# Moving a sub-block's preparation from VectorE to ScalarE and GpSimd in a row-by-row triangular solve

## What is computed

```python
probs = jax.nn.softmax(logits + causal_mask, axis=-1)
L = jnp.eye(s, dtype=probs.dtype) - jnp.tril(probs, -1)
rhs = jnp.diagonal(probs, axis1=-2, axis2=-1)[..., None] * v
A = jax.scipy.linalg.solve_triangular(L, rhs, lower=True)
```

## Time and profile before

| what | value |
|---|---|
| median of 3 runs | 1405.09 us (1400.81 to 1409.5) |
| profiled execution | 1403.81 us, span 1401.9 us |
| the four solve blocks, from the span's start | 596 to 713, 809 to 924, 1041 to 1156, 1242 to 1358 us: 463 us |
| VectorE busy in these 463 us | 388.1 us |
| TensorE busy in these 463 us | 338.8 us |
| GpSimd busy in these 463 us | 111.1 us |

### The profile page before, as it was taken

The page is one execution under the profiler, slowest core; times in us unless marked ns, Lnnn a source line. Parts: engine busy times, 40 slices in busy tenths (PEclk is TensorE's granted clock), DMA queues, the critical chain, the costliest instruction groups (busy, mean ns, idle before and its releaser), DMA issues. The chain is left out here.

```text
span 1401.9 us, 29590 instructions
## 1 busy us (share of the span) xinstructions
PE 981.4 (70%) x10762; PEld 766.5 (55%) x10762; DVE 900.0 (64%) x3559; ACT 466.1 (33%) x1066; POOL 341.8 (24%) x390
## 2 busy tenths in 40 slices
PE   5376599970665056877769968769986777986754
PEld 5165499960621034666545657646665655775643
DVE  5656262216789065888768888758878970058857
ACT  1233244424224003311235411235532126941215
POOL 1277154540047170021210021210001230012221
PEclk9788799995579587966889966789977788987877
DMA  9397598836018864410034220044411005411008
GB/s 220 46 209 210 155 249 238 228 95 180 26 50 237 244 151 123 113 28 20 21 97 129 77 61 20 22 110 125 114 46 36 24 21 163 136 45 38 28 22 235
DMA packets 241824, 153.95 MB, mean 110 GB/s; under 512 B 80432, under 2 KB 226096, under 8 KB 241424
## 3 DMA queue, kind: packets, MB, share of 16 engines
q1 hardware_dynamic: 232528, 133.04, 37.0%
q0 software_dynamic: 9152, 19.02, 4.2%
HBM read 96.76 MB, written 55.24 MB: 108 GB/s over the span
## 5 line engine op out<-in xcount | busy, mean ns | idle before, releaser
L1157 DVE TENSOR_REDUCE mx<-banks 128x1 f32<-128x384 f32 (+3 forms) x352 | 203.3, 634 | 72.6 <-PE banks L1088 72.0
L1323 DVE TENSOR_TENSOR prod<-A,Kst_Pn 128x8 f32<-128x8 f32 (+30 forms) x992 | 179.4, 221 | 0.6
L1329 DVE TENSOR_REDUCE A<-prod 128x4 f32<-128x8 f32 (+30 forms) x992 | 174.8, 217 | 0.0
L800 POOL DMA_INDIRECT o_dram<-step_o,step_to x80 | 81.4, 1017 | 309.4 <-ACT step_o L789 297.2
L1137 ACT ACTIVATE Eoff<-banks 128x256 f32<-128x256 f32 (+2 forms) x192 | 114.9, 598 | 102.6 <-PE banks L1073 93.6
L1071 PE MATMUL banks<-Qexp,Kst_Pn 128*128 128x256 bf16 x640 | 115.5, 282 | 44.1 <-DMA Qmax<-q_stack 34.0
L1139 ACT ACTIVATE Ed<-banks 128x256 f32<-128x256 f32 x256 | 98.0, 383 | 111.4 <-PE banks L1073 111.4
L1084 PE MATMUL banks<-masks,identb 128*128 128x128 bf16 (+2 forms) x352 | 90.3, 256 | 59.8 <-DMA Qmax<-q_stack 50.9
L1088 PE MATMUL banks<-Kst_Pn,Qmax 128*128 128x128 bf16 (+3 forms) x512 | 123.3, 313 | 0.0
L756 PE MATMUL banks<-step_xT,step_w 128*128 128x256 f32 x320 | 105.8, 488 | 22.5 <-issue 22.0
L1263 POOL TENSOR_TENSOR A<-A,Kst_Pn 128x256 f32<-128x256 f32 x16 | 19.4, 1213 | 408.0 <-DVE Kst_Pn L1293 408.0
(11 more groups left out here) (197 smaller groups left out, 1816.0 us busy)
## 6 DMA issues: line engine op xcount, KB each, us to landing
Kst_Pn<-k_stack SPq DMA_DIRECT2D x32, 512.0 KB, 4.6
rows_dram<-blank SPq DMA_DIRECT2D x12, 858.0 KB, 12.1
e_w<-in_L_w1T_dram SPq DMA_DIRECT2D x39, 256.0 KB
e_w<-in_L_w2T_dram SPq DMA_DIRECT2D x39, 256.0 KB
Qmax<-q_stack SPq DMA_DIRECT2D x64, 96.0 KB
Qexp<-q_stack SPq DMA_DIRECT2D x64, 96.0 KB
Kst_Pn<-k_stack SPq DMA_DIRECT2D x16, 384.0 KB, 4.5
step_xt<-rows_dram SPq DMA_DIRECT2D x40, 132.0 KB, 2.2
```

Source lines behind the costliest of these rows:

```text
L800: self.nc.gpsimd.indirect_dma_start(self.o_dram, bass.IndirectOffsetOnAxis(self.to[n][:, j:j + 1], 0), self.o[n][:, j, :], None).then_inc( ...
L1157: nc.vector.tensor_reduce(out, logits, AX_X, ALU.max, negate=True).then_inc(max_done, 1)
L1323: nc.vector.tensor_tensor(prod[:, ds, 0:r + 1], A[:, ds, k0:k0 + r + 1], Pn[:, c * SUB + r:c * SUB + r + 1, 0:r + 1].broadcast_to([P, HD / ...
L1329: nc.vector.tensor_reduce(A[:, ds, k0 + r], prod[:, ds, 0:r + 1], AX_X, ALU.add).then_inc(row_done, 1)
```

## The change

Sub-block 0 of each block is still prepared by VectorE (`first_terms`). For sub-blocks 1 to 3 the preparation is handed over: ScalarE copies the turned probabilities unscaled into `Pn` (`keep_probs`, ahead of its expert steps of the sub-block before), and GpSimd's `prepare(c + 1)`, ahead of its sends of sub-block c, makes `term`, scales all of `Pn` in one instruction of 128x1024 elements, does the own term and adds `term` to `A`. VectorE keeps the transposes and the reciprocals, but does each `turn_before` one sub-block earlier: that of sub-block 1 ahead of the rows of sub-block 0, that of c + 1 behind `keep_rows(c - 1)`. Its sums of earlier sub-blocks now go through `later` in place. New semaphores are `probs_kept` (ScalarE to TensorE and GpSimd) and `z_done` (VectorE to GpSimd). `before` and `term` have one buffer each, so VectorE waits for `own_done` before it overwrites `before`.

```diff
 def turn_next(c):
     for g in range(per_sub * c, per_sub * (c + 1)):
-        if g >= 2:
-            pe.wait_ge(probs_in, g - 1)
+        if g < 2 * per_sub:
+            pe.wait_ge(probs_in, g - per_sub + 1)
+        else:
+            pe.wait_ge(probs_kept, g - 2 * per_sub + 1)
...
 def _(act):
+    def keep_probs(c):
+        for g in range(per_sub * c, per_sub * (c + 1)):
+            act.wait_ge(probs_turned, g)
+            nc.scalar.copy(Pn[:, g * TURN:(g + 1) * TURN, :],
+                           bank[g % 2][:, 0:TURN * SUB].rearrange("p (q k) -> p q k", k=SUB)).then_inc(probs_kept, 1)
+
     for c in range(NSUB):
+        if c + 1 < NSUB:
+            keep_probs(c + 1)
         for k in tiles[c]:
...
 def _(pool):
+    own = Chain(pool, own_done)
...
+    def own_term(c):
+        ts = slice(t0 + c * SUB, t0 + (c + 1) * SUB)
+        own(nc.gpsimd.tensor_tensor(A[:, :, ts], A[:, :, ts],
+                                    diagonal(c).rearrange("p (a i) -> p a i", a=1).broadcast_to([P, HD, SUB]), ALU.mult))
+        own(nc.gpsimd.memset(diagonal(c), 1.0))
+
+    def prepare(c):
+        qs, ts = slice(c * SUB, (c + 1) * SUB), slice(t0 + c * SUB, t0 + (c + 1) * SUB)
+        z = rZ[:, qs].rearrange("p (q a) -> p q a", a=1)
+        pool.wait_ge(z_done, c)
+        own(nc.gpsimd.tensor_tensor(term[:, :, :], before[:, :, 0:HD].rearrange("p q d -> p d q"),
+                                    rZ[:, qs].rearrange("p (a q) -> p a q", a=1).broadcast_to([P, HD, SUB]), ALU.mult))
+        pool.wait_ge(probs_kept, per_sub * c)
+        own(nc.gpsimd.tensor_tensor(Pn[:, qs, :], Pn[:, qs, :], z.broadcast_to([P, SUB, SUB]), ALU.mult))
+        own_term(c)
+        own(nc.gpsimd.tensor_tensor(A[:, :, ts], A[:, :, ts], term[:, :, :], ALU.add))
+
+    pool.wait_ge(probs_in, per_sub)
+    own_term(0)
     for c in range(NSUB):
...
+        if c + 1 < NSUB:
+            prepare(c + 1)
         for k in tiles[c]:
             steps.send(pool, k)
...
 def add_later(c):
     dve.wait_ge(later_mm, c)
     base(nc.vector.transpose(later[:, :, :], wide[:, 0:SUB * HD].rearrange("p (t d) -> p d t", d=HD)))
-    add_term(c, later[:, :, :])
+    dve.wait_ge(z_done, c)
+    add_term(c, later[:, :, :], later[:, :, :], 2 + 5 * c)
+
+turn_before(0)
+first_terms()
+turn_before(1)
 for c in range(NSUB):
-    turn_before(c)
     if c:
         keep_rows(c - 1)
-    add_before(c)
-    if c:
+        if c + 1 < NSUB:
+            dve.wait_ge(own_done, 2 + 5 * c)
+            turn_before(c + 1)
         add_later(c)
-    dve.wait_ge(own_done, 2 * c + 2)
```

More of the change, by code:

```diff
@@ L1191, in solve_block @@
         sb, sem = tensors(nc, ctx)
-        own_done, base_done = sem("own_done"), sem("base_done")
+        own_done, base_done, probs_kept, z_done = sem("own_done"), sem("base_done"), sem("probs_kept"), sem("z_done")
         probs_turned, probs_in = sem("probs_turned"), sem("probs_in")
@@ L1257, in _, with diagonal @@
         def _(pool):
-            for c in range(NSUB):
[L1259 to L1266, removed]
+            own = Chain(pool, own_done)
+            def diagonal(c):
+                first = c * SUB * SUB
+                return Pn.rearrange("p q k -> p (q k)")[:, first:first + (SUB - 1) * (SUB + 1) + 1:SUB + 1]
+            def own_term(c):
[15 more added lines that the diff above has]
+            own_term(0)
+            for c in range(NSUB):
+                if c + 1 < NSUB:
+                    prepare(c + 1)
                 for k in tiles[c]:
@@ L1274, in _, with add_term, first_terms @@
             base = Chain(dve, base_done)
-            def add_term(c, sums):
+            def add_term(c, sums, out, ready):
                 qs = slice(c * SUB, (c + 1) * SUB)
                 ts = slice(t0 + c * SUB, t0 + (c + 1) * SUB)
[L1279 to L1282, removed]
+                base(nc.vector.tensor_tensor(out, sums, rZ[:, qs].rearrange("p (a q) -> p a q", a=1).broadcast_to([P, HD, SUB]), ALU.mult))
+                dve.wait_ge(own_done, ready)
+                base(nc.vector.tensor_tensor(A[:, :, ts], A[:, :, ts], out, ALU.add))
             def turn_before(c):
                 base(nc.vector.transpose(before[:, :, :], RT[:, c, :, :].rearrange("p t q -> p q t")))
-                base(nc.vector.reciprocal(rZ[:, c * SUB:(c + 1) * SUB], before[:, :, HD]))
-            def add_before(c):
-                for g in range(per_sub * c, per_sub * (c + 1)):
+                if c:
+                    nc.vector.reciprocal(rZ[:, c * SUB:(c + 1) * SUB], before[:, :, HD]).then_inc(z_done, 1)
+                else:
+                    base(nc.vector.reciprocal(rZ[:, 0:SUB], before[:, :, HD]))
+            def first_terms():
+                for g in range(per_sub):
                     gs = slice(g * TURN, (g + 1) * TURN)
@@ L1295, in add_before @@
                                             ALU.mult).then_inc(probs_in, 1)
-                add_term(c, before[:, :, 0:HD].rearrange("p q d -> p d q"))
+                add_term(0, before[:, :, 0:HD].rearrange("p q d -> p d q"), later[:, :, :], 2)
             def keep_rows(c):
```

## The result

The change makes the kernel slower: the median is 1437.29 us (1433.37 to 1440.66, four runs) against 1404.38 us (1400.81 to 1409.5) for the kernel before on the same chip, a ratio of 1.0232 (95%: 1.0204 to 1.0261). The forecast was 1433 us. The profiled execution took 1435.61 us with a span of 1433.8, 31.9 more than before; 32.05 of these lie in the four solve blocks, whose lengths (start of the block's L1313 to its last `keep_rows`) add up to 490.2 us against 458.2. The rest of the program kept its length (943.6 us against 943.7).

What follows compares the result with a forecast made beforehand. No engine filled the span; in the solve blocks VectorE's rows bound boundary 0-1 and TensorE's steps sub-block 2. Terms summed to +7.1 us per block, +28 over four, on 1403.8, plus 1.3 to the median: 1433 us, range 1412 to 1460.

Steps and rivals of the forecast that it cites:

- `turn_before(1)` ahead of the first row: Block start: the transpose for sub-block 1 now precedes the first row, with nothing covering it; +2.5 us per block.
- rows of sub-block 0: Row multiplies held by the whole of GpSimd's `prepare(1)`: +3.6 us per block, or 6.4 at the upper end.
- boundary 0-1: Between sub-blocks 0 and 1, where rows end last: `keep_rows` starts earlier, gaining 1.08 us per block.
- rows of sub-block 1: Rows held by `prepare` except `term`, which is made during the boundary: +3.1 us per block, or 5.5.
- sub-block 2 and boundary 2-3: TensorE's steps end last, with 3.9 us of slack or more covering the rows' 3.1 us: cost 0, gain 0.
- Removed from VectorE, gain 0: Boundaries: 3.05 us of scaling, waiting and adding leaves VectorE, already covered by a 2.56 us wait for TensorE; gain 0.
- GpSimd beside the rows: `prepare`'s SBUF-reading instructions hold two-input row multiplies: 4.3 us of hold, or 7.1, less 0.16 per instruction beside reduces.
- `turn_before` behind `keep_rows`: `keep_rows` no longer waits behind the transposes: gains 1.08 us at boundaries 0-1 and 1-2, 0 at 2-3.
- The new waits: Added semaphore waits on ScalarE, GpSimd, TensorE and VectorE were taken as covered: 0, or 0 to 0.1 for ScalarE's.
- the rival on the fast side: TensorE's "issue" idle time within and ahead of L1228 shrinks, without holds: 1383 us; chance 0.04.
- Without holds: Rival: GpSimd's reads do not hold the rows, which keep their length in sub-blocks 0 and 1; 1406 us, chance 0.16.
- Longer holds: Rival: GpSimd needs 1.10 us per 256 elements, holding rows longer: 12.9 us per block, 1460 us; chance 0.13.

Runs made afterwards that it cites:

- e1: Changed kernel with GpSimd's `prepare(c + 1)` moved behind its sends, waiting for the last row, so it runs at the boundary: 1413.71 us, ratio 1.007 to before.
- e2: Kernel before with two VectorE calls exchanged, `keep_rows(c - 1)` ahead of `turn_before(c)`: 1398.64 us, ratio 0.9944.
- e6: Kernel before, VectorE doing all its work, with each `turn_before` one sub-block earlier: 1412.82 us, ratio 1.0039.
- e4: Kernel before plus four idle GpSimd copies of 128x1024 beside the rows of each of sub-blocks 0 and 1: 1428.53 us, ratio 1.0139.
- e5: Kernel before plus four idle GpSimd memsets of 128x1024, reading nothing, beside the rows of each of sub-blocks 0 and 1: 1405.53 us, ratio 0.9993.
- e7: Changed kernel with `prepare` moved to the boundary, the same kernel run again unchanged on another chip: 1415.86 us, ratio 1.0049 to before.

## Why the prediction was right, step by step

The sums over four blocks, after less before, from the timelines of the two profiled executions:

| step of the prediction | forecast, us | measured, us |
|---|---|---|
| `turn_before(1)` ahead of the first row | +10.0 | +10.1 |
| rows of sub-block 0 | +14.4 | +12.6 |
| boundary 0-1 | -4.3 | -0.6 |
| rows of sub-block 1 | +12.4 | +10.3 |
| boundary 1-2 | -4.3 | -4.0 |
| sub-block 2 and boundary 2-3 | 0 | +3.1 |
| sub-block 3 | 0 | +0.6 |
| sum | +28.2 | +32.1 |

**Removed from VectorE, gain 0.** Right for boundary 0-1, where e1 and e2 show it together, as told there. In the kernel before, VectorE waits for TensorE ahead of L1305 at all twelve boundaries, 1.83 us at the least, so the work was covered there too; only where `keep_rows` goes first is it exposed at some of the boundaries 1-2.

**`turn_before` ahead of the first row, 2.5 us.** Right: 2.52 us a block (8.97 against 6.45), and e6 gives 2.59 with GpSimd out of it.

**GpSimd beside the rows.** The mechanism is shown, by e1 from the side of place, by e4 and e5 from that of reading. The sum of the lengths was right, its parts were not. GpSimd's groups by line after (busy, mean ns, idle before):

```profile
L1287 POOL TENSOR_TENSOR Kst_Pn<-Kst_Pn,rZ 128x1024 f32<-128x1024 f32 x12 | 22.9, 1912 | 68.0 <-ACT Kst_Pn L1252 67.7
...
L1284 POOL TENSOR_TENSOR later_term<-before,rZ 128x256 f32<-128x256 f32 x12 | 10.2, 846 | 70.2 <-DVE rZ L1315 70.2
L1289 POOL TENSOR_TENSOR A<-A,later_term 128x256 f32<-128x256 f32 x12 | 8.8, 732 | 1.0
```

With L1276, whose median is 0.86 us, that is 0.85 + 1.91 + 0.86 + 0.73 = 4.35 us of hold, where I had 3 x 0.69 + 2.2 = 4.3. That the sums agree is luck: the three short instructions were 0.37 us longer together than forecast, and the scaling 0.29 shorter than the 2.2 worked out from them. Nor was 0.69 the right reading of L1263: the same multiplication takes 0.86 beside the rows (L1276), so of its 1.10 in the earlier trace rows some 0.24 were waiting, not 0.41.

What each costs the rows was sized too high, and this is the term that was off: I let 0.16 us of each go beside the reduces, and the rows of sub-block 0 grew by 3.16 us for 4.35 of hold, so that 0.30 of each is free (0.39 of e4's copies, 1.05 - 2.65 / 4). The rows show where the rest is. A held pair of multiplies ends 0.11 to 0.17 us behind GpSimd's instruction (means by line over the 40 held pairs of after), while an unheld one takes 0.25 to 0.32: some 0.15 of the pair's own length is not added either. The earlier trace rows had this already: L1426 ended 0.55 us behind GpSimd's copy and takes 0.69 alone. With the 0.16 between two pairs this makes the 0.30; it is more where GpSimd starts just before the pair ahead ends (L1287 and L1276 by 0.07, the copies by 0.09) and less where it starts late (L1289, 0.12 behind it). Why a held pair ends so soon was not tried and stays open. All this made the rows of sub-blocks 0 and 1 cheaper than forecast, by 3.9 us over the four blocks.

**Sub-block 2, cost 0.** Right in kind, off in size. Its rows grew by 2.47 us, and in all blocks the steps still ended last, 1.8 to 3.6 us behind the rows. In block 0 after, `turn_rows` starts at 690.03, and `keep_rows` waits 4.58 us for it:

```profile
690.03 1.04 PE L1220 MATMUL banks<-ident_c,A 128*96 128x128 f32 x8
...
691.10 1.06 DVE L1332 COPY Apos<-banks 32x512 f32<-32x512 f32 x1 [4.58 <-PE banks L1220]
```

The +3.1 us come from the steps: +1.95, -1.96, +0.64 and +2.44 us in the four blocks. Between two executions of one program, e1 and e7, sub-block 2 differs by 2.35, 0.06, 2.50 and 1.86 us, so I take the sum for that scatter; whether the change makes the slow `down` more frequent isn't settled by one profile each.

**`turn_before` behind `keep_rows`, 1.08 us.** Right as a mechanism (`keep_rows` followed `turn_rows` 4.5 us earlier over the four blocks, at 0-1, and 4.1 at 1-2; e2 has the gain alone). It fails at 0-1 in this kernel: `turn_rows` takes 7.6 us in place of 4.2, +3.4, and from `keep_rows` to the transpose of the sums it takes 0.6 more. The prediction foresaw that TensorE would be idle here for several us, since the rows are 3.2 us longer and start 2.5 us later beside steps that keep their length; it put nothing in the sum for the low granted clock behind that. The runs show it with and without holds: at 0-1 of block 0 `turn_rows` took 1.05 us behind 2.57 us of idle time (e2), 1.58 and 1.89 behind 4.94 (e1 and e7, without holds), 1.89 behind 6.16 (after). The two errors, -3.9 on the rows and +3.7 at this boundary, cancel by luck; the 4 us by which the sum falls short are nearly all in sub-blocks 2 and 3.

**The new waits, cost 0.** Right: outside the blocks' starts (1.08 us for L1278 in block 0, where the kernel before waited 0.88 for L1263; the difference is in the 2.5) VectorE has no idle time for `own_done`. TensorE's "issue" gaps inside the products, the rival on the fast side, stayed: 1.74 us at boundary 0-1 of block 0 after, ahead of the last 48 matmuls of L1230.

**The rivals.** Without holds the rows would have kept their length; they did so only where no reading GpSimd instruction stood beside them, in e1 and e7 (1.007 and 1.0049 of before), e2 (0.9944), e5 (0.9993) and e6 (1.0039). Longer holds needed 1.10 us for 256 elements and 3.8 for the scaling; 0.73 to 0.86 and 1.91 were measured. The kernel that beats both before and after is e2.

## What to carry to other kernels

Before handing work from VectorE to GpSimd, look at what VectorE does at the receiving place: beside instructions with two SBUF inputs a GpSimd instruction that reads SBUF costs VectorE nearly its whole length (here 0.3 to 0.4 us less), and work that was hidden behind another wait brings nothing in return. Where a wait ends late, first look at the order of what stands ahead of the instruction that is waited for: here two calls exchanged gave 0.6%, and moving the work cost 2.3%. When one engine's stretch gets longer, check the granted clock of the engine that then stands idle, since its first work afterwards can take nearly twice as long.

## What the runs showed of the hardware that I had not expected

- A GpSimd memset leaves VectorE's two-input multiplies alone (e5), yet one seems to hold a one-input instruction at the program's start. In before, L136 took 0.84 us and ended at 10.33, just behind a memset that ended at 10.31; the next instance took 0.17:

```profile
6.81 3.50 POOL L1532 MEMSET pad<- 16x4096 bf16 x1
...
9.49 0.84 DVE L136 TENSOR_SCALAR n_rstd<-n_mv 128x4 f32<-128x4 f32 x1
...
10.88 0.17 DVE L136 TENSOR_SCALAR n_rstd<-n_mv 128x4 f32<-128x4 f32 x1
```

  The first L136 does so in all nine traces: it takes 0.84 to 1.04 us, depending on when it starts, and ends 0.03 us behind the memset. No run was made with the memset moved. The Trainium skill (SBUF — State Buffer, section "SBUF: two separate sides") has VectorE operations in a 2-port mode contend with any GpSimd operation, which would fit if L136 ran in such a mode; no run here shows whether it did.
- The reduces of the rows, with one input, were not held by GpSimd's instructions: 176.5 us in all after against 174.8 before.
- GpSimd's multiplies of 256 elements took 0.85 us (L1284, L1276), its addition of as many 0.73 (L1289), and the scaling of 1024 elements 1.91, so 1.87 ns an element. The operation and the order in which the inputs lie differ at once, so which of them makes the addition shorter is not shown.
